# One order of work per pair, the Wout product in fp32 on row halves, and the attention in the bank of s

## What is computed

```python
xn = layernorm(x)
# ffn, M = 64 channels, INNER = 16
s = xn @ Win + bin_                                # rows x 64
h = relu(s[..., None] * W1 + b1)                   # rows x 64 x 16
g = einsum('btmh,mh->btm', h, W2) + b2             # rows x 64
ffn = g @ Wout + bout                              # rows x 512
# attention, 16 heads of 32: q, k, v from xn, then three rounds of
#   linear maps of a head's 32 features, layernorms, softmax over positions
# with a choice of round 1's or round 2's result by the mean difference
out = x + attn @ Wo.T + bo + ffn
```

## Time and profile before

| | us |
|---|---|
| median of 3 runs (376.67 to 378.64) | 377.44 |
| the profiled execution | 375.8 |
| its span, first to last instruction | 373.7 |
| TensorE busy | 337.0 (90%) |
| VectorE busy | 282.9 (76%) |
| ScalarE busy | 278.2 (74%) |
| GpSimd busy | 237.3 (64%) |
| DMA | 73.02 MB, mean 195 GB/s |
| granted TensorE clock, mean | 0.990 |

### The profile page before, as it was taken

One profiled execution on the slowest core, in us unless ns is written; L12 is line 12 of the kernel. 1 busy time (PEld: TensorE's weight loads), 2 busy tenths in 40 slices (PEclk: granted clock), 3 DMA queues, 4 the chain that ended last, 5 costly groups with the idle time before them and its releaser, 6 DMA issues.

```text
span 373.7 us, 5638 instructions
## 1 busy us (share of the span) xinstructions
PE 337.0 (90%) x1964; PEld 161.1 (43%) x1964; DVE 282.9 (76%) x507; ACT 278.2 (74%) x366; POOL 237.3 (64%) x209
## 2 busy tenths in 40 slices
PE   2489889789997998898999999999999999999774
PEld 2274554345533553444444444444434444443322
DVE  0677757888788799987969687877878787877664
ACT  0363568785786677867998999998989898988820
POOL 8405385992767649839094949494949585769900
PEclk9999989999999999999999999999999999999998
DMA  8999303334346425653575757576756652223647
GB/s 254 266 383 348 117 3 113 112 114 125 157 168 227 153 100 198 224 170 128 216 275 205 263 205 269 203 260 224 280 211 249 224 224 114 113 114 140 208 157 296
DMA packets 15052, 73.02 MB, mean 195 GB/s; under 512 B 4121, under 2 KB 4273, under 8 KB 6833
## 3 DMA queue, kind: packets, MB, share of 16 engines
q1 hardware_dynamic: 12304, 72.23, 53.1%
q0 software_dynamic: 640, 0.16, 0.8%
q10 hardware_dynamic: 2080, 0.28, 0.8%
HBM read 38.96 MB, written 33.69 MB: 194 GB/s over the span
## 4 chain that ended last, share of the span: by engine, by line
PE 63%; POOL 10%; DVE 8%; ACT 6%; issue 5%; DMA 5%; SPq 1%; POOLq 0%; DVEq 0%; ACTq 0%
PE op L443 14%; PE T L377 14%; PE g L425 13%; PE s L387 12%; POOL o L867 7%; DMA o<-in_L_attn_Wv_dram 5%; PE rep L410 4%; ACT H L541 3%; DVE stats L788 2%; PE g L396 1%; POOL rstd L842 1%; DVE o L763 1%; ACT G L551 1%; PE op L276 1%; DVE SH L774 1%
## 5 line engine op out<-in xcount | busy, mean ns | idle before, releaser
L867 POOL TENSOR_TENSOR o<-x,bias_row 128x512 f32<-128x512 f32 x128 | 164.1, 1319 | 4.0 <-issue 4.0
L541 ACT ACTIVATE H<-rep,b1c,w1c 128x1024 f32<-128x1024 f32 x128 | 153.6, 1206 | 14.5 <-PE rep L410 13.7
L763 DVE TENSOR_TENSOR o<-o,op 128x512 f32<-128x512 f32 x128 | 86.9, 682 | 39.3 <-PE op L443 38.3
L513 ACT ACTIVATE xT<-T 128x512 f32<-128x512 f32 x128 | 76.2, 596 | 39.7 <-PE T L377 39.2
L377 PEld LDWEIGHTS T<-ident,x 128*128 128x128 f32 x512 | 54.9, 142 | 107.4 <-issue 75.9
L377 PE MATMUL T<-ident,x 128*128 128x128 f32 x512 | 84.9, 289 | 11.6 <-DMA x<-in_L_attn_x_dram 9.1
L788 DVE BATCH_NORM_STATS2 stats<-x 128x6 f32<-128x512 f32 x128 | 83.2, 682 | 0.4
L842 POOL TENSOR_TENSOR rstd<-veps,nhalf 128x8 f32<-128x8 f32 x16 | 26.4, 1651 | 83.9 <-DVE veps L798 83.9
L387 PE MATMUL s<-xT,win 128*64 128x512 f32 x256 | 70.5, 630 | 0.0
L425 PE MATMUL g<-H,w2s 128*32 128x512 f32 x512 | 68.2, 605 | 0.4 <-ACT H L541 0.4
L443 PE MATMUL op<-wout_hi,G 128*128 128x512 f32 x128 | 62.7, 490 | 5.9 <-DVE G L781 3.7
(11 more groups left out here) (166 smaller groups left out, 246.5 us busy)
## 6 DMA issues: line engine op xcount, KB each, us to landing
x<-in_L_attn_x_dram SPq DMA_DIRECT2D x32, 1024.0 KB, 6.8
out_dram<-o SPq DMA_DIRECT2D x32, 1024.0 KB, 4.3
o<-in_L_attn_Wq_dram SPq DMA_DIRECT2D x1, 1024.0 KB, 14.6
o<-in_L_attn_Wk_dram SPq DMA_DIRECT2D x1, 1024.0 KB, 16.4
o<-in_L_attn_Wv_dram SPq DMA_DIRECT2D x1, 1024.0 KB, 19.4
o<-in_L_attn_Wo_dram SPq DMA_DIRECT2D x1, 1024.0 KB, 19.2
H<-in_L_ffn_Wout_dram SPq DMA_DIRECT2D x2, 128.0 KB, 14.7
bias_row<-in_L_ffn_bout_dram SPq DMA_DIRECT2D x1, 256.0 KB, 12.1
```

The source lines that it names most:

```text
L513: act.activation(xT[:, c, b * BLK:(b + 1) * BLK], T_ps[k % 2][:, :], ACT.Copy).then_inc(ev_done, 1)
L541: act.activation(Hr[half][k % len(Hr[half])][:, :], rep_ps[:, :], ACT.Relu, bias=b1c[:, half, k:k + 1], scale=w1c[:, half, k:k + 1]).then_ ...
L763: dve.tensor_tensor(o_sb[m][:, c], o_sb[m][:, c], product_bank(n, j), ALU.add).then_inc(add_done, 1)
L867: pool.tensor_tensor(o_sb[m][:, c], x_sb[m][:, c], bias_row[:, :], ALU.add).then_inc(xc_done, 1)
```

## The change

PSUM: o_ps becomes one tensor of two banks, all of it for the product with Wout; the attention moves to the bank of s (`A_ps = s_ps`). TensorE's attention steps wait, where they first enter the bank in a body, for the scaling of the pair before (`claim`), and `s_product` waits for the last reader (`bank_read`).

The fp32r split of g and Wout goes: `evacuate_g` is one ScalarE instruction of 128x512 per pair, `g_low`, wout_hi and wout_lo are gone. G holds the pair's first half in partitions 0 to 63, its second in 64 to 127. `project` has four steps per pair, each two fp32 products with 64 contraction rows at array rows 0 and 64, into one bank each; `add` has four steps of 128x1024, covering row tiles j and j + 4. Stores are by the parts i = 0, 1 (row tiles 0, 1, 4, 5, then 2, 3, 6, 7), biases are added in the order 0, 4, 1, 5, 2, 6, 3, 7, and a load waits for 7 or 8 biases instead of 4 or 8.

Transposes go half by half (four chunks of half 0, then of half 1) instead of chunk by chunk; groups 1 and 5 are evacuated by VectorE. The order of each engine is written out per body (pair), 16 ticks, with N + 3 bodies. The attention's rounds begin at tick 72 and are 48 apart; turns are at the ticks of `TURN_AT`. The head loads pair 0, the biases, pair 1, then Wq, Wk, Wout, Wv, Wo, pair 2, and after these, on SP's queue, the 13 small parameters that ScalarE's queue had issued.

```diff
-        T_ps, s_ps, g_ps, o_ps, rep_ps = [ps("T0"), ps("T1")], ps("s"), ps("g"), [ps("op0"), ps("op1")], ps("rep", 2)
+        T_ps, s_ps, g_ps, o_ps, rep_ps = [ps("T0"), ps("T1")], ps("s"), ps("g"), ps("op", 2), ps("rep", 2)
...
-        A_ps = o_ps[1]
-        banks = [rep_ps[:, 0:D], rep_ps[:, D:2 * D], o_ps[0][:, :]]
+        A_ps = s_ps
+        banks = [o_ps[:, 0:D], o_ps[:, D:2 * D]]
...
+        BODIES = N + 3
+        BY_DVE, BY_ACT = (1, 5), (0, 2, 3, 4, 6, 7)
+        BIAS_ORDER = (0, 4, 1, 5, 2, 6, 3, 7)
+        TURN_AT = (21, 22, 23, 24, 26, 27, 29, 31, 32, 33, 34, 35, 36, 37, 39, 41)
+        FIRST_ROUND, ROUND = 72, 48
...
+            for i, w in enumerate((Wv, Wo)):
+                sp.dma_start(w_nat[2 + i], w.rearrange("(c p) i -> p c i", p=P)).then_inc(in_w[2 + i], 16)
             load(2, 0)
             load(2, 1)
-            for n in range(-2, N):
+            for i, w in enumerate((Wlq, Wlk, Wlv)):
+                sp.dma_start(small[:, i * HD:(i + 1) * HD], w).then_inc(in_small, 16)
...
+            for n in range(2, BODIES):
+                if has(n - 3):
+                    store(n - 3, 0)
                 for h in range(2):
-                    if n >= 0:
-                        store(n, h)
-                    if RING <= n + 5 < N:
-                        load(n + 5, h)
-
+                    if has(n + 1):
+                        load(n + 1, h)
+                if has(n - 3):
+                    store(n - 3, 1)
...
+        def claim(tick):
+
+            pe.wait_ge(s_done, tick // TICKS)
...
+        def s_product(n):
+            if n == 0:
                 pe.wait_ge(win_centred, 1)
-            pe.wait_ge(ev_done, SLOTS * n + 2 * c + 2)
-            if n > 0 and c == 0:
+            else:
                 pe.wait_ge(s_done, n)
-            for b in range(2):
-                mm = pe.matmul(s_ps[b * M:(b + 1) * M, :], win[:, c, :], xT[:, c, b * BLK:(b + 1) * BLK],
-                               start=(c == 0), stop=(c == DC - 1))
-            mm.then_inc(sc_done, 1)
+            pe.wait_ge(ev_act, len(BY_ACT) * (n + 1))
+            pe.wait_ge(ev_dve, len(BY_DVE) * (n + 1))
+            if bank_read:
+                pe.wait_ge(*bank_read)
+            for c in range(DC):
+                for b in range(2):
+                    mm = pe.matmul(s_ps[b * M:(b + 1) * M, :], win[:, c, :], xT[:, c, b * BLK:(b + 1) * BLK],
+                                   start=(c == 0), stop=(c == DC - 1))
+                mm.then_inc(sc_done, 1)
...
-            for part in (wout_hi, wout_lo):
-                mm = pe.matmul(product_bank(n, j), G[m][:, j * P:(j + 1) * P], part[:, :], start=(part is wout_hi), stop=(part is wout_lo))
+            if TILES * n + j > 0:
+                pe.wait_ge(add_done, TILES * n + j)
+            for b in range(2):
+                own = slice(b * M, (b + 1) * M)
+                mm = pe.matmul(o_ps[:, b * D:(b + 1) * D], G[n % 2][own, j * P:(j + 1) * P], wout[own, :],
+                               start=True, stop=True, tile_position=(b * M, 0))
             mm.then_inc(op_done, 1)
...
+            act.activation(G[n % 2][:, :], g_ps[:, :], ACT.Identity, bias=b2c[:, 0:1]).then_inc(g_made, 1)
...
+            both = by_tile(o_sb[m][:, :], j)
+            dve.tensor_tensor(both, both, o_ps[:, :].rearrange("p (h d) -> p h d", h=2), ALU.add).then_inc(add_done, 1)
```

More of the change, by code:

```diff
@@ L13 @@
 RING = 3
-SLOTS = 8
+TICKS = 16
 EPS = 1e-5
@@ L227, in sp_program @@
             load(0, 1)
[L228 to L231, removed]
-            sp.dma_start(wo2[0:M, :], Wout).then_inc(in_wo2, 16)
-            sp.dma_start(wo2[M:P, :], Wout).then_inc(in_wo2, 16)
             sp.dma_start(bias_row[:, :], bout.partition_broadcast(P)).then_inc(in_rows, 16)
@@ L399, in replicate @@
         def replicate(n, half):
-            if n == 0:
-                pe.wait_ge(turn_dve, 8)
-                pe.wait_ge(turn_act, 8)
+            if n == 0 and half == 0:
                 pe.wait_ge(spread_made, 1)
@@ new lines, in act_program @@
+            for n in range(BODIES):
+                t = TICKS * n
+                reach(side, t)
+                if has(n):
+                    evacuate(n, 0)
+                if has(n - 2):
+                    relu(n - 2, 4)
+                reach(side, t + 1)
+                if has(n):
+                    evacuate(n, 2)
+                if has(n - 1):
+                    copy_rstd(n - 1)
+                reach(side, t + 2)
+                if has(n - 2):
+                    relu(n - 2, 5)
+                reach(side, t + 3)
+                if has(n - 1):
+                    s_high(n - 1)
+                reach(side, t + 4)
+                if has(n - 2):
+                    relu(n - 2, 6)
+                reach(side, t + 5)
+                if has(n - 2):
+                    relu(n - 2, 7)
+                reach(side, t + 6)
+                if has(n):
+                    evacuate(n, 3)
+                reach(side, t + 7)
+                if has(n):
+                    evacuate(n, 4)
+                reach(side, t + 8)
+                if has(n - 2):
+                    evacuate_g(n - 2)
+                reach(side, t + 9)
+                if has(n):
+                    evacuate(n, 6)
+                reach(side, t + 10)
+                if has(n):
+                    evacuate(n, 7)
+                reach(side, t + 11)
+                for r in range(HK):
+                    if has(n - 1):
+                        relu(n - 1, r)
+                    reach(side, t + 12 + r)
@@ L591, in dve_attention @@
             yield 0
+            dve.wait_ge(ident_made, 2)
+            v = tick(dve.tensor_tensor(isum[:, :], ident[:, 0:M], ident[:, M:P], ALU.add))
+            dve.wait_ge(dve_own, v)
+            v = tick(dve.tensor_tensor(istack[:, :], isum[:, 0:MH], isum[:, MH:M], ALU.add))
+            for half in range(2):
+                ins = dve.tensor_copy(spread[:, half, :].rearrange("p (g m) -> p g m", g=HG),
+                                      isum[:, half * MH:(half + 1) * MH].unsqueeze(1).to_broadcast([P, HG, MH]))
+            ins.then_inc(spread_made, 1)
+            yield 1
             dve.wait_ge(wsum, 1)
```

531 lines of the change are left out of this document (296 added, 235 removed).

## The result

The changed kernel takes 386.1 us (median of four runs, 385.2 to 388.5), the kernel before on the same chip 378.0. The ratio is 1.022, with an interval of 1.017 to 1.027: longer and clear of no change (though not clear of 2%), where 355 us and faster was forecast. The profiled execution took 388.5 us with a span of 386.7.

The account below looks back on a forecast made before the run. TensorE was taken to bound the kernel: 61 for the head through body 2, 13 x 17.0 for settled bodies, 35 attention and 34.5 tail give a span of 351.5; plus 3.7 around it, 355 us, range 338 to 378.

Parts of the forecast that it names:

- GpSimd stands last in no step: Settled body: a pair's last biases are done at 2.5 us of the next body; loads behind have 14 us for 6.8.
- Body 3: Body making the attention's block matrices: 17.0 us plus 4 us of attention.
- The settled body: Pair without attention: TensorE's 16.2 us of work plus a 0.9 us wait, about 17.0 us.
- The forecast wait: TensorE ahead of project(3): waits 0.9 us for VectorE's add(2), as the product has no second buffer.
- TensorE's own work: Per pair: transposes 3.8, replications 1.0, products 4.0, sum_h 1.0 + 2.75, s 3.6, together 16.2 us.
- The rounds' sum: Attention after body 3: three rounds of 8.3 us make 25, selection +4, last product +1.9.
- s_product for vT: Body with lin and kv: s waits 1.6 us because kT and vT lie behind four statistics on VectorE.
- the logits for q's scaling: In each round, qs_made comes at 11.0 while TensorE is there at 8.7: 2.3 us wait, scaling taking 1.34.
- The tail: Last bodies: body 16 about 13.2 us, body 17 21 with four product-and-add steps of 2.4; sum 34.5 us.
- pure gain: Head: moving 13 of ScalarE's 18 transfers to SP lets ScalarE evacuate early, at no cost; first evacuation near 8 us.
- Rival 3: Wout row halves run one after the other, 1.74 us a step instead of 0.88: 405 us, slower; chance 0.10.
- Rival 2: VectorE's chain becomes the bound, attention bodies 1.5 us longer and the rest 0.3: 374 us; chance 0.15.

Follow-up runs that it names:

- h1_inv_std_first: Changed kernel, with GpSimd making pair 1's inverse deviation ahead of pair 0's biases in body 1: 375.2 us, ratio 0.998 to the kernel before.
- kv_one_tick_earlier: Changed kernel, with kT and vT of a round on VectorE behind two statistics instead of four: 382.9 us, ratio 1.018 to the kernel before.
- last_pair_two_buffers: Changed kernel, with products 1 and 3 of the last pair in the replication's two banks: 380.9 us, ratio 1.012 to the kernel before.
- add2_before_stats: Changed kernel, with VectorE's add(2) ahead of the third statistics instead of behind it: 384.3 us, ratio 1.023 to the kernel before.
- before_with_parameters_on_sp: Kernel before, with the 13 small parameters issued on SP's queue ahead of pair 2's loads instead of on ScalarE's: 376.6 us, ratio 1.001.
- h12e_biases_held: Changed kernel, inverse deviations of pairs 1 and 2 ahead of biases, VectorE's constants in body 2, body 3's biases held for both s_low: 370.7 us, ratio 0.989.
- all_mended_biases_held_always: Changed kernel with all head, kT/vT, add(2) and last-pair edits, and biases held for s_low in every body from 3 on: 394.1 us, ratio 1.046.

## Why the prediction was wrong

The forecast span was 351.5, the profile's is 386.7. Taken stretch by stretch, with the first transposes of a body as its border, the 35.2 us are these:

| stretch | forecast | profile | difference |
|---|---|---|---|
| body 0 | 22.5 | 24.8 | 2.3 |
| body 1 | 14.5 | 14.5 | 0 |
| body 2 | 24 | 36.2 | 12.2 |
| body 3 | 17 + 4 | 28.6 | 7.6 |
| bodies 4 to 15 | 12 x 17 + 31 | 243.1 | 8.1 |
| tail | 34.5 | 39.6 | 5.1 |

**The step that failed** is the sentence "GpSimd stands last in no step". It was worked out for a settled body and applied to all. I had even put pair 0's biases late in the head ("45 or later"), to say that SP's queue is not late; but I did not ask what stands behind those biases on GpSimd itself. It is pair 1's inverse deviation, and behind that pair 2's, on which TensorE's spread waits. This is 10.5 us of direct waits (9.0 and 1.5) and some more of lower clock. Of the 31 us between forecast and measurement it is the largest single part, and it makes the difference between slower and level: h1_inv_std_first, with nothing else changed, is level with the kernel before instead of 2.2% slower. It does not bring the forecast gain back; the other 22 us are in the stretches below.

**Body 3** was sized at 4 us of attention. It has a second wait that I did not have: small VectorE instructions on SBUF tiles take about one bias of GpSimd longer when they stand beside biases. The constants cost 3.3 us instead of 0.7, add(2) was late by it, TensorE waited 3.1 us and went on at the lower clock (a product of 2.08 us). Moving the constants was worth 5 us. The lower clock belongs to this execution: in h1_inv_std_first, kv_one_tick_earlier and last_pair_two_buffers the same wait of 3.1 us is followed by a product of 1.13, and pairs 2 and 3 are 21.4 us apart instead of 24.1. So 2.6 of the 7.6 us are not the rule.

**The settled body**: 17.73 us against 17.0. The forecast wait is there, in its place, but smaller:

```profile
334.10 1.09 PE L439 MATMUL T<-ident,x 128*128 128x128 f32 x8
335.52 1.13 PE L506 MATMUL op<-wout,G 64*128 64x512 f32 x4 [0.33 <-DVE o L875]
```

```profile
326.25:343.98 17.73, 17.19 (x108) 7.62 (x104) 14.19 (x22) 14.55 (x19) 12.59 (x10) 1.00 0.30 120
```

The product is held by add(2) for 0.33 us; 0.9 was forecast. TensorE's own work was the term mis-sized: it is busy 17.2 us between the two marks, and not 16.2, and with add(2) out of its way (add2_before_stats) the body is still 17.45. Counted from start to start, four products are 4.2 for 4.0, the transposes about 4.4 for 3.8 (a group ahead of a change of shape 0.53 instead of 0.42), the two replications 1.15 for 1.0. And sum_h 0 waits 0.21 us for ScalarE's copy of R, a wait that I had passed over. Of the forecast gain of 0.9 us a pair, 0.17 was left.

**The rounds' sum** was right, in part by luck: bodies 4 to 15 are 30.3 us above twelve times 17.73, forecast 31. The waits of TensorE that belong to the attention, over the whole run:

```profile
PE s L453 <- DVE vT L816: 4.0, 3, 1.3
PE s L361 <- DVE qT L852: 3.3, 2, 1.6
PE s L396 <- DVE qk L833: 2.9, 3, 1.1
PE s L453 <- DVE xn L868: 2.3, 1, 2.3
```

Three of them stand where the walk through the ticks had put them, and all three are smaller: s_product for vT 4.0 us (forecast 4.8), the logits for q's scaling 2.9 (forecast 6.9, as the scaling took 0.35 us and not 1.34), the selection 2.3 (forecast 4). The second row, 3.3 us ahead of the linear maps of rounds 2 and 3, was in no term. There two s_low beside biases hold VectorE:

```profile
173.03 2.86 DVE L893 TENSOR_TENSOR SH<-s_full,SH 64x512 fp32r<-64x512 f32 x2
```

They are 1.4 us by themselves. So the contention that the sum had left out shows in the rounds too, and waits too large made up for it.

**The tail** was right in its chain, product and add in turn. It was 5 us longer: the four steps with their lower clock in the last products (11.5 us for 9.6), the waits of rep for s_low and ScalarE's relus in body 16 (1.4), and the start of body 17 (8.9 us for 7.2; a product of pair 14 took 2.08 us and the first sum 1.44 there).

**The head's "pure gain"** was none in the kernel before, by before_with_parameters_on_sp. Body 1 came out at 14.5 as forecast; body 0 was longer as s ran at the lower clock for most of its time, 6.5 us for 4.5.

Of the signs named, the first evacuation (7.9 us) and the steps of 1.06 us came; marks 17.0 us apart, a wait of 0.9 and pair 15's mark near 313 did not (17.73, 0.33, 344.0). Of the rivals none was this one. Rival 3 (row halves in series) fell: a step is 1.06 us, four records of 671 ns. Rival 2 named VectorE's chain and would have given 374; its mechanism, hand-overs between product and add, is a part of what the drain showed, but did not bind the settled bodies. The rival that was missing is a queue that is in order and waits, in the head, for something that has nothing to do with the instructions behind.

## To carry to other kernels

When an order is rewritten, walk each engine's queue in the bodies that differ from the settled one, too: for every wait that only the first bodies have, write down what stands behind it on that engine and who waits for that. A step of work that sits on the critical loop (here the inverse deviation) belongs ahead of bulk work on a queue that may block. A single buffer between two engines costs little in a full pipeline and its whole round trip in the drain, where an idle buffer of an earlier stage can serve as the second.

## What the runs showed of the hardware

VectorE's instructions that read two tensors from SBUF are held by GpSimd's elementwise ones: 0.17 us becomes 1.22 to 1.31 beside biases of 1.24 us, and two s_low of 1.4 us together took 2.9 beside a row of 6, and 3.1 and 7.3 beside rows of 14. Adds from PSUM (1.22 us) and statistics (0.68) keep their time in the same stretches. The Trainium skill, GPSIMD Engine Reference, Specifications, says that the SBUF interfaces are shared with VectorE, with contention for instructions that have two SBUF inputs; the traces agree, and add the size in this kernel: often about one instruction of GpSimd, at worst several. avg, with one input and a constant, suffered as well (1.30 for 0.21); the page's other case, a mode that uses both ports, may be that, which no run here shows. Holding GpSimd back does not remove the contention, it moves it: to nat in h12e_biases_held, to the variance in all_mended_biases_held_always.

TensorE's granted clock fell after single waits, and not each time: after 9.0 us transposes took 1.06 instead of 0.60 us, after 3.0 and 3.1 us a product took 2.08 in two profiles and 1.13 in others, and after a wait of 2.3 us s_product took 5.35 instead of 3.65 in some profiles and 3.65 in others of the same stretch. So a wait of 2.3 us can cost 4.0 (2.3 and the 1.7 of s_product behind it), and two executions of one stretch can differ by this alone.
